# A gated expert layer on one core: other early loads, and two token halves turned by VectorE in 32x32 blocks

## The reference, cut to what matters

```python
# x: (8, 128, 128) float32 tokens; E = 8 experts, D = 128, F = 512; gates g (8, 8), shared gate sg (8,)
g = jnp.einsum('bsd,edf->ebsf', h, Wg)
u = jnp.einsum('bsd,edf->ebsf', h, Wu)
expert_outs = jnp.einsum('ebsf,efd->ebsd', jax.nn.silu(g) * u, Wd)
expert_output = jnp.einsum('be,ebsd->bsd', gating_probs, expert_outs)
shared = jnp.einsum('bsf,fd->bsd', jax.nn.silu(h @ Sg) * (h @ Su), Sd)
return x + (1.0 - sg) * expert_output + sg * shared
```

## Time and profile before

| | us |
|---|---|
| median of three runs | 161.5 |
| lowest, highest | 161.22, 162.55 |
| the profiled execution, its time | 161.85 |
| its span in the trace | 160.1 |
| TensorE busy | 155.2 (97%) |
| ScalarE busy | 108.3 (68%) |
| VectorE busy | 98.4 (61%) |
| GpSimd busy | 79.7 (50%) |

### The profile page before, as it was taken

How to read it: one execution, slowest core, us unless ns; L and a number is a source line. 1 busy time by engine, 2 the same in 40 slices (tenths; PEclk the granted TensorE clock), 3 DMA queues, 4 the chain that set the end, 5 groups by cost and what they waited for, 6 DMA issues and landing times.

```text
span 160.1 us, 2319 instructions
## 1 busy us (share of the span) xinstructions
PE 155.2 (97%) x679; PEld 126.2 (79%) x679; DVE 98.4 (61%) x159; ACT 108.3 (68%) x200; POOL 79.7 (50%) x81
## 2 busy tenths in 40 slices
PE   6799999999999999999999999999999999999992
PEld 1687788888888888888888888888888888888872
DVE  0448578676666666666666666656665666666672
ACT  3337885877577766776677667766777687755540
POOL 4354998255825582557255735473547354740000
PEclk9999999999999999999999999999999999999999
DMA  4956006000600060005000500051000000000003
GB/s 140 206 187 186 10 0 196 5 0 2 199 0 0 2 195 6 0 0 196 1 0 0 186 10 0 0 166 31 0 0 0 0 0 0 0 0 4 0 3 129
DMA packets 8134, 8.24 MB, mean 51 GB/s; under 512 B 560, under 2 KB 5424, under 8 KB 8128
## 3 DMA queue, kind: packets, MB, share of 16 engines
q1 hardware_dynamic: 7776, 7.74, 15.3%
q0 software_dynamic: 64, 0.04, 1.0%
q10 hardware_dynamic: 288, 0.39, 0.7%
HBM read 7.64 MB, written 0.52 MB: 51 GB/s over the span
## 4 chain that ended last, share of the span: by engine, by line
PE 95%; DMA 2%; DVE 0%; issue 0%
PE y_ps L453 10%; PE y_ps L448 10%; PE y_ps L450 10%; PE u_ps L539 9%; PE g_ps L536 9%; PE g_ps L534 9%; PE u_ps L541 9%; PE u_ps L540 9%; PE g_ps L535 9%; DMA x_nat<-in_x 2%; PE g_ps L509 1%; PE u_ps L515 1%; PE g_ps L511 1%; PE g_ps L508 1%; PE u_ps L518 1%; PE u_ps L516 1%
## 5 line engine op out<-in xcount | busy, mean ns | idle before, releaser
L371 DVE TENSOR_TENSOR h_ps<-silu,u_ps 128x512 f32<-128x512 f32 x71 | 49.4, 697 | 49.6 <-PE u_ps L541 45.4
L295 ACT ACTIVATE h_hi<-h_ps 128x512 fp32r<-128x512 f32 x71 | 42.6, 600 | 39.7 <-DVE h_ps L371 39.7
L232 POOL TENSOR_TENSOR w_lo<-w_raw,w_hi 128x384 fp32r<-128x384 f32 x32 | 32.5, 1018 | 37.6 <-ACT w_hi L285 37.6
L376 DVE TENSOR_TENSOR h_lo<-h_ps,h_hi 128x512 fp32r<-128x512 f32 x71 | 48.5, 684 | 0.1
L290 ACT ACTIVATE silu<-g_ps 128x512 f32<-128x512 f32 x72 | 42.9, 597 | 2.0 <-PE g_ps L480 2.0
L237 POOL TENSOR_TENSOR xs_lo<-xs,xs_hi 128x512 fp32r<-128x512 f32 x16 | 20.6, 1290 | 16.1 <-ACT xs_hi L281 16.1
L453 PE MATMUL y_ps<-h_lo,w_hi 128*128 128x512 f32 x71 | 27.9, 392 | 0.0
L448 PE MATMUL y_ps<-h_hi,w_lo 128*128 128x512 f32 x71 | 27.7, 390 | 0.0
L450 PE MATMUL y_ps<-h_hi,w_hi 128*128 128x512 f32 x71 | 27.6, 389 | 0.0
L534 PE MATMUL g_ps<-x_hi,w_hi 128*128 128x512 f32 x64 | 24.9, 389 | 0.0
L535 PE MATMUL g_ps<-x_lo,w_hi 128*128 128x512 f32 x64 | 24.9, 389 | 0.0
(11 more groups left out here) (79 smaller groups left out, 124.0 us busy)
## 6 DMA issues: line engine op xcount, KB each, us to landing
w_raw<-in_L_cond_Wg SPq DMA_DIRECT2D x8, 256.0 KB, 2.7
w_raw<-in_L_cond_Wu SPq DMA_DIRECT2D x8, 256.0 KB, 3.1
w_raw<-in_L_cond_Wd SPq DMA_DIRECT2D x8, 256.0 KB, 4.0
w_raw<-in_L_cond_Sg SPq DMA_DIRECT2D x1, 256.0 KB, 3.7
x_nat<-in_x ACTq DMA_DIRECT2D x1, 256.0 KB, 3.9
w_raw<-in_L_cond_Su SPq DMA_DIRECT2D x1, 256.0 KB, 4.0
x_nat<-in_x SPq DMA_DIRECT2D x1, 256.0 KB, 4.2
w_raw<-in_L_cond_Sd SPq DMA_DIRECT2D x1, 256.0 KB, 7.9
```

Source lines behind the costliest of these rows:

```text
L295: act.activation(h_hi[k % HB][:, :], h_ps[k % BANKS][:, :], ACT.Copy)\
L371: dve.tensor_tensor((to or h_ps[k % BANKS])[:, :], silu[k % BANKS][:, :], u_ps[k % BANKS][:, :], ALU.mult).then_inc(hidden_done, 1)
L376: dve.tensor_tensor(h_lo[k % HB][:, :], h_ps[k % BANKS][:, :], f32(h_hi[k % HB][:, :]), ALU.subtract).then_inc(h_lo_done, 1)
```

## The change

The early loads. SyncE's queue now begins with the first token half, then Sg and Su, then the second token half in four loads, one for each 32 columns, then the two gate tensors, then expert 0. Sd moves to ScalarE's queue, behind the load of its function table. GpSimd issues no transfer. The matmuls on zeros are five of 512 columns and one of 256 at the start, and one of 256 in place of two of 512 between.

The second token half. Its four loads put block column c of the tokens (32 of the 128 model columns) on partitions 32c to 32c+31, in pieces of 128 bytes, so that a transpose of each 32x32 block on VectorE gives the whole transpose, `x_t` of that half, in SBUF. TensorE's four transposes at L497 are gone. ScalarE makes the hi part behind silu of unit 2, and GpSimd the lo part, ahead of its wait for the coefficients. GpSimd's sum for that half is not needed any more. Unit 4 takes the three gate matmuls in another order, the one with the lo part last.

The first output half. VectorE's add moves to unit 5 of the last expert, and at unit 6 it turns the half in 32x32 blocks; SyncE stores it in four transfers in pieces of 128 bytes. TensorE's four transposes and ScalarE's copy of 512 columns are gone.

The last stores. The fourth token block of the second half goes to the free bank `y_ps[0]`; ScalarE copies blocks 0 and 1, then 3, VectorE copies block 2. The two stores stay as they were in size and in queue.

```diff
@@ -14,10 +14,11 @@
...
 HB = 4
+BLK = 32
+NAT = [(0, 0), (0, 1), (1, 0), (2, 0)]
 GATE, UP, DOWN = range(3)
 DMA = 16
-WARM_UP = 6
-WARM_BETWEEN = 2
+WARM_UP = 5
@@ -49,7 +50,10 @@
...
-        x_nat = sbuf("x_nat", [P, HALVES, NQ, D], FP32)
+        x_nat = sbuf("x_nat", [P, NQ, D], FP32)
+        x_blk = sbuf("x_blk", [P, N], FP32)
         x_t = sbuf("x_t", [P, HALVES, N], FP32)
@@ -74,7 +78,10 @@
...
         y_t = sbuf("y_t", [P, HALVES, N], FP32)
-        out_sb = sbuf("out_sb", [P, HALVES, NQ, D], FP32)
+
+
+        y_blk = sbuf("y_blk", [P, N], FP32)
+        out_sb = sbuf("out_sb", [P, NQ, D], FP32)
@@ -152,16 +162,22 @@
...
         def _(sp):
+            sp.dma_start(x_nat[:, :, :], x_view[0]).then_inc(x_loaded[0], DMA)
             sp.dma_start(w_raw[0][:, GATE, :, :], in_slices(Sg)).then_inc(first_w_loaded[GATE], DMA)
             sp.dma_start(w_raw[0][:, UP, :, :], in_slices(Su)).then_inc(first_w_loaded[UP], DMA)
-            sp.dma_start(x_nat[:, 1, :, :], x_view[1]).then_inc(x_loaded[1], DMA)
-            sp.dma_start(w_raw[0][:, DOWN, :, :], in_rows(Sd)).then_inc(first_w_loaded[DOWN], DMA)
+            for c in range(P // BLK):
+
+                of = x_view[1][:, :, c * BLK:(c + 1) * BLK].rearrange("(s j) q d -> j q s d", j=BLK)
+                sp.dma_start(x_blk[c * BLK:(c + 1) * BLK, :].rearrange("j (q s d) -> j q s d", q=NQ, d=BLK), of)\
+                  .then_inc(x_loaded[1], DMA)
...
+            sp.dma_start(sg_sb[:, :], shared_gate.partition_broadcast(P)).then_inc(sg_loaded, DMA)
+            sp.dma_start(gates_sb[:, :, :], gates.partition_broadcast(P)).then_inc(gates_loaded, DMA)
             load_expert(0, 1)
@@ -176,13 +192,18 @@
...
-            sp.wait_ge(first_half_ready, 1)
-            sp.dma_start(out_view[0], out_sb[:, 0, :, :]).then_inc(out_stored[0], DMA)
+            sp.wait_ge(y0_turned, 1)
+            for c in range(P // BLK):
+
+                to = out_view[0][:, :, c * BLK:(c + 1) * BLK].rearrange("(s j) q d -> j q s d", j=BLK)
+                sp.dma_start(to, y_blk[c * BLK:(c + 1) * BLK, :].rearrange("j (q s d) -> j q s d", q=NQ, d=BLK))\
+                  .then_inc(blocks_stored[c], DMA)
             sp.wait_ge(nat_copied[0], 1)
-            sp.dma_start(out_view[1][:, 0:HALF_Q, :], out_sb[:, 1, 0:HALF_Q, :]).then_inc(out_stored[1], DMA)
+            sp.dma_start(out_view[1][:, 0:HALF_Q, :], out_sb[:, 0:HALF_Q, :]).then_inc(out_stored[0], DMA)
+            for c in range(P // BLK):
+                sp.wait_ge(blocks_stored[c], DMA)
             sp.wait_ge(out_stored[0], DMA)
             sp.wait_ge(out_stored[1], DMA)
-            sp.wait_ge(out_stored[2], DMA)
@@ -190,8 +211,6 @@
...
                                base=0, pattern=[[-1, P]], channel_multiplier=1).then_inc(ident_built, 1)
-            pool.dma_start(sg_sb[:, :], shared_gate.partition_broadcast(P)).then_inc(sg_loaded, DMA)
-            pool.dma_start(gates_sb[:, :, :], gates.partition_broadcast(P)).then_inc(gates_loaded, DMA)
@@ -207,19 +226,19 @@
...
-            def whole_tokens(h):
-
-                pool.wait_ge(x_hi_done, h + 2)
-                pool.wait_ge(x_lo_done, h + 2)
-                pool.tensor_tensor(x_t[:, h, :], f32(x_hi[:, h, :]), f32(x_lo[:, h, :]), ALU.add)\
+            def whole_tokens():
+
+                pool.wait_ge(x_hi_done, 2)
+                pool.wait_ge(x_lo_done, 2)
+                pool.tensor_tensor(x_t[:, 0, :], f32(x_hi[:, 0, :]), f32(x_lo[:, 0, :]), ALU.add)\
                     .then_inc(x_t_done, 1)
...
                 for h in range(HALVES):
-                    if first:
-                        whole_tokens(h)
-                        pool.wait_ge(x_t_done, h + 1)
-                    else:
+                    if first and h == 0:
+                        whole_tokens()
+                        pool.wait_ge(x_t_done, 1)
+                    elif not first:
@@ -239,6 +258,10 @@
...
+
+            pool.wait_ge(x1_hi_done, 1)
+            pool.tensor_tensor(x_lo[:, 1, :], x_t[:, 1, :], f32(x_hi[:, 1, :]), ALU.subtract)\
+                .then_inc(x1_lo_done, 1)
@@ -255,10 +278,9 @@
...
         def _(act):
-            act.dma_start(x_nat[:, 0, :, :], x_view[0]).then_inc(x_loaded[0], DMA)
-
...
             act.activation(table[:, :], zeros[:, 0:1], ACT.Silu)
+            act.dma_start(w_raw[0][:, DOWN, :, :], in_rows(Sd)).then_inc(first_w_loaded[DOWN], DMA)
@@ -273,8 +295,8 @@
...
             def second_x_hi():
-                act.wait_ge(x_transposed, 3)
-                act.activation(x_hi[:, 1, :], y_ps[1][:, :], ACT.Copy).then_inc(x_hi_done, 1)
+                act.wait_ge(x1_turned, 1)
+                act.activation(x_hi[:, 1, :], x_t[:, 1, :], ACT.Copy).then_inc(x1_hi_done, 1)
@@ -316,10 +338,11 @@
...
             hidden_hi(0, 0)
-            second_x_hi()
             hidden_hi(1, 1)
...
                 silu_of(k, k)
+                if k == BANKS:
+                    second_x_hi()
                 split_next(k, 1, 0, 1)
@@ -330,15 +353,16 @@
...
-            act.wait_ge(y0_transposed, 1)
-            act.activation(out_sb[:, 0, :, :], g_ps[0][:, :].rearrange("p (q d) -> p q d", q=NQ), ACT.Copy)\
-               .then_inc(first_half_ready, 1)
+
             act.wait_ge(nat_done, 1)
-            act.activation(out_sb[:, 1, 0:HALF_Q, :],
+            act.activation(out_sb[:, 0:HALF_Q, :],
                            nat_ps[0][:, 0:HALF_N].rearrange("p (q d) -> p q d", q=HALF_Q), ACT.Copy)\
                .then_inc(nat_copied[0], 1)
+            act.wait_ge(nat_done, 3)
+            act.activation(out_sb[:, NQ - 1, :], nat_ps[2][:, 0:D], ACT.Copy).then_inc(nat_copied[2], 1)
             act.wait_ge(nat_copied[1], 1)
-            act.dma_start(out_view[1][:, HALF_Q:NQ, :], out_sb[:, 1, HALF_Q:NQ, :]).then_inc(out_stored[2], DMA)
+            act.wait_ge(nat_copied[2], 1)
+            act.dma_start(out_view[1][:, HALF_Q:NQ, :], out_sb[:, HALF_Q:NQ, :]).then_inc(out_stored[1], DMA)
@@ -385,9 +409,8 @@
...
             hidden_lo(0, 0)
-            dve.wait_ge(x_hi_done, 3)
-            dve.tensor_tensor(x_lo[:, 1, :], y_ps[1][:, :], f32(x_hi[:, 1, :]), ALU.subtract)\
-               .then_inc(x_lo_done, 1)
+            dve.wait_ge(x_loaded[1], DMA * (P // BLK))
+            dve.transpose(x_t[:, 1, :], x_blk[:, :]).then_inc(x1_turned, 1)
             dve.wait_ge(sg_loaded, DMA)
@@ -413,11 +436,14 @@
...
                 hidden_lo(UNITS * E + k - 1, (k - 1) % UNITS)
-                if k == UNITS - 2:
+                if k == NF + 1:
                     dve.wait_ge(down_done, LAST + 1 - NF)
...
                        .then_inc(y0_ready, 1)
+                if k == NF + 2:
+                    dve.wait_ge(y0_ready, 1)
+                    dve.transpose(y_blk[:, :], y_t[:, 0, :]).then_inc(y0_turned, 1)
             hidden_lo(LAST - 1, UNITS - 2)
@@ -427,18 +453,17 @@
...
             dve.wait_ge(nat_done, 2)
-            dve.tensor_copy(out_sb[:, 1, HALF_Q:NQ, :],
-                            nat_ps[1][:, 0:HALF_N].rearrange("p (q d) -> p q d", q=HALF_Q))\
-               .then_inc(nat_copied[1], 1)
+            dve.tensor_copy(out_sb[:, HALF_Q, :], nat_ps[1][:, 0:D]).then_inc(nat_copied[1], 1)
...
         def _(pe):
-            def warm(n):
-                for _ in range(n):
-                    pe.matmul(u_ps[1][:, :], zeros[:, 0:P], zeros[:, :], start=True, stop=True)
+            def warm(cols):
+                pe.matmul(u_ps[1][:, 0:cols], zeros[:, 0:P], zeros[:, 0:cols], start=True, stop=True)
             pe.wait_ge(zeros_set, 1)
-            warm(WARM_UP)
+            for _ in range(WARM_UP):
+                warm(N)
+            warm(HALF_N)
             pe.wait_ge(ident_built, 1)
@@ -458,10 +483,10 @@
...
                 for q in range(HALF_Q):
-                    last = pe.transpose(first_ps[i][:, q * P:(q + 1) * P], x_nat[:, 0, i * HALF_Q + q, :],
+                    last = pe.transpose(first_ps[i][:, q * P:(q + 1) * P], x_nat[:, i * HALF_Q + q, :],
                                         ident[:, :])
                 last.then_inc(x_transposed, 1)
-            warm(WARM_BETWEEN)
+            warm(HALF_N)
@@ -491,24 +516,19 @@
...
-
-            pe.wait_ge(x_loaded[1], DMA)
-            for q in range(NQ):
-                last = pe.transpose(y_ps[1][:, q * P:(q + 1) * P], x_nat[:, 1, q, :], ident[:, :])
-            last.then_inc(x_transposed, 1)
-
...
                 if k == NF:
-                    pe.wait_ge(x_hi_done, 3)
-                    pe.wait_ge(x_lo_done, 3)
+                    pe.wait_ge(x1_hi_done, 1)
                 pe.wait_ge(silu_done, k - BANKS + 1)
...
                 pe.matmul(g[:, :], w_hi[0][:, GATE, f, :], x_hi[:, h, :], start=True, stop=False)
-                pe.matmul(g[:, :], w_hi[0][:, GATE, f, :], x_lo[:, h, :], start=False, stop=False)
                 pe.wait_ge(first_pool_lo, 1)
-                pe.matmul(g[:, :], w_lo[0][:, GATE, f, :], x_hi[:, h, :], start=False, stop=True)\
```

(60 more changed lines are left out.)

## The result

The changed kernel's median was 160.17 us (20 executions, 159.98 to 161.17), that of the kernel before 161.95 (20 executions beside it, 160.92 to 162.55). The ratio is 0.9917, 95% interval 0.9901 to 0.9934: 0.8% faster, some 1.3 us. The forecast was 161.3 with 0.2 us gained. The time lies in the forecast range and within 1% of 161.3, but the kernel moved by several times what was forecast, and by more than its measurement is uncertain.

The account below looks back on a forecast made before the run. TensorE was taken as full except at the two ends, which bound the kernel. Start -1.30, GpSimd's delay +1.37 and end -0.25 sum to -0.2 against the median 161.5: 161.3 us, range 159.7 to 163.0.

Parts of the forecast that it names:

- The matmuls of units 0 and 1: Start: tokens first let real matmuls begin 1.30 us earlier; with seven of twelve steps still slow, L491 ends at 9.59.
- the bound of 8.80: Start: earliest end forecast for L491, if the clock rises after three slow steps, 2.09 us earlier than before.
- Sd: Start: Sd, moved to ScalarE's queue and issued near 2.7 us, would cause no wait.
- GpSimd's delay: Start: x_lo ahead of x_t on GpSimd delays x_t and unit 6 by 1.37 us relative to E, L491's end.
- The forecast wait of over 1 us before unit 6: Start: TensorE would wait over 1 us for h_lo before unit 6.
- L497's 0.44: Start: dropping L497's four transposes, 0.44 us, gains nothing; unit 4 starts at E+4.72 both times, E being L491's end.
- The block transpose: VectorE's block transpose of 512 columns takes 0.68 us, bounds 0.34 and 1.36.
- Small pieces: Token loads and end stores: a 128-byte piece takes 27 ns, bounds 12 and 48, so 0.25 of the end's 0.8 us is kept.
- The break-even of 32 ns: End: above 32 ns per 128-byte piece, the first half's stores would end past the old 159.6 us.
- Expert 0's load: Start: expert weights follow the token pieces by 3.2 us, at 12.8; ScalarE can wait until 14.8, so hidden.
- Rival 2: Start and end: clock rises after three steps and small pieces are cheap, -1.5 us, so 160.0; chance 0.23.

Follow-up runs that it names:

- e11: Changed kernel with three full matmuls on zeros at the start in place of five; median 161.46 us, ratio 0.9975 to the kernel before.
- e3: Kernel before with eight matmuls on zeros at the start in place of six; median 161.47 us, ratio 0.9968 to the kernel before.
- e6: Kernel before with the gate loads on SyncE's queue behind Sd and eight matmuls on zeros in place of six; median 159.90 us, ratio 0.9872.
- e1: Kernel before with only the change's new end; median 161.19 us, ratio 0.9957 to the kernel before.
- e4: Changed kernel with GpSimd's sum x_t of the first half moved ahead of its wait for the second half's hi part; median 159.44 us, ratio 0.9858 to the kernel before.
- e9: Changed kernel with the second token half again loaded in one transfer and turned by TensorE, GpSimd's sums in old order; median 159.01 us, ratio 0.9829 to kernel before.
- e2: Changed kernel with the old end; median 160.94 us, ratio 0.9964 to the kernel before.
- e7: e4 with the two gate loads moved from SyncE's queue to ScalarE's behind Sd; median 159.03 us, ratio 0.9813 to the kernel before.
- e8: Changed kernel with the two gate loads back on GpSimd's queue; median 160.40 us, ratio 0.9908 to the kernel before.

## Why the prediction was wrong, step by step

**The matmuls of units 0 and 1: the step that failed.** "If seven of its twelve steps stay slow, L491 ends at 9.59." Less than two of the twelve were slow and it ended at 8.30, 1.29 before the forecast and beyond the bound of 8.80. Of this, 0.44 is the tokens: they landed at 3.54 instead of 4.02 (at the head of the queue they take 2.8, so the loop's 2.7 was a better row than bytes counted under a crowded start), and the first real matmul began at 5.01 instead of 5.45. The other 0.85 is the missing slow steps, worth 1.05, less 0.20 in which TensorE waited for Su's cast (ahead of the pair L509 at 6.64), a wait that the prediction didn't have. I had the mechanism among the rivals (no idle time before the tokens) and argued against it from a trace that had that idle time, which says nothing about a kernel without it. The kernel with the idle time put back (e11) loses 0.9 us, and the kernel before with it filled (e3, e6) runs fast from the transposes on. That filling the idle time brings the rise forward is shown, as a matter of more executions and not of none and all: e1's trace has the idle time and an early rise. The Trainium skill (TensorE: Matmul & The Clock Gate, Part 1) says that the throttled clock is the default and that activity releases it; these runs agree.

**Sd: right for the change, overlooked for the kernel before.** I wrote that Sd would cost no wait, and it didn't (landed 5.3). It was also issued at 1.18 and not near 2.7: ScalarE's queue didn't hold it behind the table load, which ran from 0.74 to 2.02. What I missed is that in the kernel before it was a second bound only 0.25 under the first. The trace had it: the cast ended at 10.51, the first product began at 10.76. That is why on the kernel before the warm-up alone gives 0.3%, the gate loads off GpSimd's queue alone 0.5 to 0.7% and both 1.3%. It didn't make the forecast wrong, but a reader of the forecast would have tried the warm-up alone.

**GpSimd's delay: right, to 0.1.** Forecast 1.37 later relative to E, measured 1.47; unit 6 at E+10.48 against E+10.37. With this the change gives back 1.48 of the 2.59 that it gains at the start, and e4's last store comes 0.96 earlier and e9's 1.45, in both with a part that isn't GpSimd's (0.08 and 0.20 are an earlier E, and in e9 an earlier Wd). The forecast wait of over 1 us before unit 6 came as 0.59 before unit 5 and 0.45 before unit 6. That L497's 0.44 was hidden behind unit 1's h_lo held exactly (E+4.72 in both).

**The block transpose: right.** 0.70 against 0.68 taken; the 1.24 estimated from the Trainium skill (VectorE: DVE Perf Modes, The three transpose paths) doesn't hold for 512 float32 columns in one instruction.

**Small pieces: a term mis-sized.** 27 ns taken, 12.9 (loads) and 13.7 (stores) measured, on the line through the two known sizes. So 0.67 of the end was kept and not 0.25, close to the full 0.8; the block stores were 0.9 clear of the last one, and the missing 0.13 lies in the twelve small matmuls (1.43 instead of 1.34) and in the copy (0.36 to the issue instead of 0.46, where 0.15 was forecast). I had taken the nearest row where the line was the better guide. The break-even of 32 ns was wrong by the prediction's own terms: 154.65 and 128 pieces and 1.25 reach 159.6 at 29 ns. The Trainium skill (DMA: Bandwidth & Descriptors, Specifications) says that under 512 bytes the rate isn't full: 128 bytes in 12.9 ns are 9.9 GB/s an engine, against 19 for 512 bytes in 27, so that much agrees; a price as high as a 512-byte piece's, which I drew from it, is not seen.

**Expert 0's load: the number right by luck, and not hidden.** Wd landed at 12.57 (forecast 12.8), but not for the bytes and pieces that the forecast added up. Pieces cost half of what it took, and from 6.5 to 9 us the engines were 12% busy; the load came late because SyncE needed until 7.3 to issue it, a term the forecast didn't have. ScalarE waited 1.07 for it, and through silu and h_lo so did TensorE before unit 5 (0.59). It cost nothing only because GpSimd's chain set unit 6 in any case, and it became the bound as soon as that chain was shortened (e4).

**Sum.** -2.59+1.48-0.67 = -1.78, the span's 1.8; forecast -1.30+1.37-0.25. Rival 2 (clock early, pieces cheap) was what happened. That its 160.0 is close to the measured 160.17 is luck in part, and so is that the time lies well within the range: -1.78 from the 161.5 of three executions would be 159.7, the range's lower end, but the kernel before measured 161.95 this time.

What stays open: whether it is the idle time itself or what TensorE does in its place, and what else decides the rise, since e2 without idle time rose later than the others and e1 with it early. Nine of the changed kernel's twenty executions took 160.3 to 161.2 and eleven 160.0 to 160.2, which would fit a later rise in some of them, but only one execution of it has a trace.

## What to carry to other kernels

Where a chain of waits stays on one engine at the start, look for what ends just before it on the others: a second bound within 0.3 us of the first hides what lifting the first would give, and a pair of small edits can beat a large one (e6 against the change). Before an operation is moved from an engine that looks full to an idle one, list what stands behind it in that queue and whether it could have gone ahead: x_lo ahead of x_t delayed xs by 1.5 us, and the order of two GpSimd lines was worth 1.0. Count the issues too: four small loads ahead of a large one held it back by their 2.8 us of SyncE's time. Fill an idle TensorE with matmuls on zeros up to the moment that its first operand lands, and check it by the durations of the steps.

## What the runs showed of the hardware that I had not expected

Pieces of 128 bytes cost 13 to 14 ns of one transfer engine, loads and stores alike, and loads' came at up to 1700 per us. A transfer with them takes 0.62 to 0.74 us of its sequencer instead of 0.43, and the issue of a 256 KB load right behind four of them took 2.9 us (e7) and 2.45 (e8). With two tiny transfers on GpSimd's queue, a 256 KB load in SyncE's queue landed 7.5 to 8.3 us after its issue, without them 4.6 to 5.2; on ScalarE's queue it didn't matter (4.2 and 4.1, e8). The same start ran at 0.43 or at 0.23 us per 512 columns, and it stayed longer at 0.43 in most traces in which TensorE had idled for 0.6 to 1.1 us before its first real work (three of four), against none of nine without.
